# A decoder block on one core: two of three normalisations move to ScalarE, the split of the cross queries to GpSimd, the row of maxima to the head of VectorE's step, and a stack's transfers to other places in SyncE's list

## The reference

```
x = x + attn(layernorm(x))            # 16 heads of 8 channels, rotary positions, causal
x = x + xattn(layernorm(x), context)  # 16 heads over 256 context tokens, then W_proj and bias
x = x + ffn(layernorm(x))             # 8 experts, 2 chosen per batch from the mean over tokens
layernorm(x) = (x - mean) / sqrt(var + 1e-5)
ffn: hmid = gelu(h @ w1[e] + b1[e]); y = hmid @ w2[e] + b2[e]; out += weight[b, e] * y
```

## Time and profile before

| | |
|---|---|
| median of 3 runs | 202.76 us |
| profiled execution | 200.95 us, span 199.2 us |
| mean granted clock of TensorE | 0.947 of full speed |
| busy: PE / PEld / DVE / ACT / POOL | 84% / 58% / 71% / 53% / 26% |
| chain that ended last | PE 50%, DVE 19%, DMA 15%, SPq 5% |

### The profile page before, as it was taken

The page is one execution under the profiler, slowest core; times in us unless marked ns, Lnnn a source line. Parts: engine busy times, 40 slices in busy tenths (PEclk is TensorE's granted clock), DMA queues, the critical chain, the costliest instruction groups (busy, mean ns, idle before and its releaser), DMA issues.

```text
span 199.2 us, 4411 instructions
## 1 busy us (share of the span) xinstructions
PE 166.8 (84%) x1500; PEld 116.1 (58%) x1508; DVE 140.7 (71%) x545; ACT 104.8 (53%) x222; POOL 52.3 (26%) x103
## 2 busy tenths in 40 slices
PE   0686195699599979989998998998998899799994
PEld 0343184485466755755764655654665556598984
DVE  2789299897347899799799889888968346525020
ACT  2132021257147656566566666766676657793451
POOL 7810005668800070030030030010115107126050
PEclk9999669589769999999999999999999999999999
DMA  5817660058227503322321321300340350170720
GB/s 150 238 35 175 164 173 18 3 148 184 70 82 196 184 25 104 110 69 58 109 82 49 98 95 35 90 0 3 113 130 3 100 143 0 17 224 26 229 66 26
DMA packets 23842, 19.05 MB, mean 96 GB/s; under 512 B 2364, under 2 KB 21820, under 8 KB 23100
## 3 DMA queue, kind: packets, MB, share of 16 engines
q1 hardware_dynamic: 22908, 17.79, 31.9%
q10 hardware_dynamic: 912, 0.98, 2.0%
HBM read 12.54 MB, written 2.49 MB: 75 GB/s over the span
## 4 chain that ended last, share of the span: by engine, by line
PE 50%; DVE 19%; DMA 15%; SPq 5%; issue 4%; POOL 3%; ACT 2%; POOLq 0%; DVEq 0%; ACTq 0%
PE psV L914 11%; PE psB L893 9%; PE psA L868 8%; DMA stackQ<-maxT 6%; DMA stackQ<-scratch 4%; DVE masked L623 4%; PE psA L958 4%; PE psM L923 3%; PE psA L975 3%; DMA stackK<-hid 3%; PE psV L975 3%; PE psM L933 3%; DVE stats L554 2%; DVE negmax L629 2%; SPq L402 2%
## 5 line engine op out<-in xcount | busy, mean ns | idle before, releaser
L753 ACT ACTIVATE E<-psB 128x512 f32<-128x512 f32 x112 | 62.3, 595 | 37.3 <-PE psB L893 15.7
L868 PE MATMUL psA<-stackK,stackQ 72*128 72x256 bf16 (+1 forms) x256 | 44.4, 277 | 11.8 <-DMA stackK<-hid 5.5
L893 PE MATMUL psB<-stackQ,stackK 74*128 74x256 bf16 (+1 forms) x256 | 42.2, 264 | 4.6 <-DMA stackQ<-maxT 3.8
L623 DVE CUSTOM_DVE_ANT_0 masked<-psA,row_mask 128x128 bf16<-128x128 f32 (+1 forms) x128 | 36.8, 352 | 11.8 <-PE psA L868 11.7
L629 DVE TENSOR_REDUCE negmax<-psA 128x2 f32<-128x512 f32 x64 | 39.7, 677 | 0.0
L868 PEld LDWEIGHTS psA<-stackK,stackQ 72*128 72x128 bf16 x256 | 23.0, 105 | 21.5 <-DMA stackQ<-scratch 8.6
L914 PE MATMUL psV<-E,V 128*9 128x256 f32 (+1 forms) x512 | 30.9, 359 | 0.2 <-ACT E L753 0.2
L893 PEld LDWEIGHTS psB<-stackQ,stackK 74*128 74x128 bf16 x256 | 22.0, 100 | 12.5 <-DMA stackQ<-maxT 5.6
L468 POOL TENSOR_SCALAR rstd<-mv 128x2 f32<-128x2 f32 x12 | 2.8, 236 | 89.1 <-DVE mv L558 88.9
L914 PEld LDWEIGHTS psV<-E,V 128*9 128x9 f32 x512 | 11.0, 90 | 14.4 <-issue 7.9
L761 ACT ACTIVATE oT<-psV 128x256 f32<-128x256 f32 x32 | 12.3, 384 | 7.9 <-PE psV L914 7.2
(11 more groups left out here) (111 smaller groups left out, 247.0 us busy)
## 6 DMA issues: line engine op xcount, KB each, us to landing
stackK<-scratch SPq DMA_DIRECT2D x18, 192.0 KB
stackQ<-hid SPq DMA_DIRECT2D x36, 64.0 KB
w1s<-w_dram SPq DMA_DIRECT2D x8, 258.0 KB, 2.8
w2s<-w_dram SPq DMA_DIRECT2D x8, 256.0 KB, 3.7
stackQ<-scratch SPq DMA_DIRECT2D x3, 576.0 KB
stackK<-hid SPq DMA_DIRECT2D x18, 64.0 KB
scratch<-hid SPq DMA_DIRECT2D x4, 192.0 KB, 3.7
scratch<-parts_ctx SPq DMA_DIRECT2D x4, 192.0 KB, 4.7
```

The costliest lines, as they stand in the source:

```text
L623: last = dve.tensor_tensor_reduce(out=masked[:, bank, i * keys:(i + 1) * keys], in0=scores[:, i, 0:keys], in1=row_mask[:, S - keys:S], sca ...
L753: act.activation(dst, psB[:, bank].rearrange("p (h q) -> p h q", h=dst.shape[1]), ACT.Exp, scale=SCALE).then_inc(b_taken, 1)
L868: last = pe.matmul(psA[:, bank, i * keys:(i + 1) * keys], stackQ[0:ROWS, b, h, t * P:(t + 1) * P], stackK[0:ROWS, b, h, 0:keys], start=Tru ...
L893: last = pe.matmul(psB[:, bank, i * n:(i + 1) * n], stackK[:, b, h, t * P:(t + 1) * P], stackQ[:, b, h, q0:S], start=(s == 1 or i == 0), s ...
```

## The change

1. `ln_apply` of the second and third normalisation (s > 0) moves from VectorE to ScalarE, as Identity(res * rstd + shift). GpSimd makes shift = -mean * rstd in two more operations on two columns, one ahead of rstd and one behind it. The first normalisation stays.
2. The cross queries are copied out of psM by ScalarE (new buffer qc) and split by GpSimd, four operations; VectorE's four go.
3. `max_rows` is cut in two. TensorE's turn (`max_turn`) stays behind the half's units. VectorE's split and SyncE's transfer (`max_rows`) come ahead of them.
4. `o_turn`, `o_back`, `o_proj`, `ln_stats` and `ln_apply` come one half earlier; `ln_turn`, `q_cross`, `stack_read_k` and the routing keep their half.
5. Writes and reads of the stacks of batches 2 and 3 are steps of their own for keys and queries. The third batch's keys are written ahead of the first row of maxima, and both stacks are read ahead of the second batch's row of maxima.
6. The masked scores have two buffers instead of three.

```diff
--- before.py
+++ after.py
...
@@ -95,6 +95,7 @@
     put(5, "qk_self", 0, 3)
     put(6, "v_cross", 1, 1)
     put(7, "ctx_turn", 1, 2)
+    put(7, "max_turn", 0, 0)
     put(7, "max_rows", 0, 0)
...
@@ -102,9 +103,14 @@
...
-    put(9, "stack_write", 0, 2)
-    put(10, "stack_read", 0, 2)
-    put(14, "stack_write", 0, 3)
+    put(6, "stack_write", 0, 2, 1)
+    put(9, "stack_write", 0, 2, 0)
+    put(9, "stack_read", 0, 2, 1)
+    put(10, "stack_read", 0, 2, 0)
+    put(13, "stack_write", 0, 3, 1)
+    put(14, "stack_write", 0, 3, 0)
+    put(14, "stack_read", 0, 3, 1)
+    put(15, "stack_read", 0, 3, 0)
...
@@ -114,24 +120,22 @@
         s, b = divmod(j, NB)
         n = 2 * NG * j
         if j > 0:
-            put(n + 2 * NG, "max_rows", s, b)
-        if j == 1:
-            put(n + 2 * NG + 1, "stack_read", 0, 3)
-        m = n + LAG + 10
+            row_of[n + 2 * NG] = (s, b)
+        m = n + LAG + 9
         put(m, "o_turn", s, b)
         put(m + 1, "o_back", s, b)
         put(m + 2, "o_proj", s, b)
         put(m + 2, "ln_stats", s + 1, b)
         put(m + 3, "ln_apply", s + 1, b)
-        put(m + 4, "ln_turn", s + 1, b)
+        put(m + 5, "ln_turn", s + 1, b)
         if s == 0:
-            put(m, "stack_read_k", 1, b)
-            put(m + 5, "q_cross", 1, b)
-            put(m + 5, "stack_fill", 1, b)
+            put(m + 1, "stack_read_k", 1, b)
+            put(m + 6, "q_cross", 1, b)
+            put(m + 6, "stack_fill", 1, b)
...
@@ -153,13 +157,17 @@
...
+        if half in row_of:
+            order.append(("max_rows", *row_of[half]))
         order += [step for _, step in sorted(units, key=lambda unit: unit[0])]
+        if half in row_of:
+            order.append(("max_turn", *row_of[half]))
...
@@ -224,7 +232,7 @@
-        masked = sb("masked", [P, NA, 2 * S], BF16)
+        masked = sb("masked", [P, 2, 2 * S], BF16)
...
@@ -237,6 +245,8 @@
+        qc = sb("qc", [P, 2, S])
+        shift = sb("shift", [P, NB, NT])
...
@@ -379,16 +390,17 @@
...
-                if kind == "stack_write" and s == 0:
-                    sp.wait_ge(parts_k_self[b], NPART)
-                    write_parts(0, b, 1, parts[:, b, 1], scr_k_self[b])
-                    sp.wait_ge(parts_q_self[b], NPART)
-                    write_parts(0, b, 0, parts[:, b, 0], scr_q_self[b])
-                if kind == "stack_read" and s == 0:
-                    sp.wait_ge(scr_k_self[b], 16)
-                    read_k(s, b)
-                    sp.wait_ge(scr_q_self[b], 16)
-                    read_q(s, b)
+                if kind == "stack_write":
+                    which = st["g"]
+                    sp.wait_ge((parts_q_self[b], parts_k_self[b])[which], NPART)
+                    write_parts(s, b, which, parts[:, b, which], (scr_q_self[b], scr_k_self[b])[which])
+                if kind == "stack_read":
+                    which = st["g"]
+                    sp.wait_ge((scr_q_self[b], scr_k_self[b])[which], 16)
+                    if which == 1:
+                        read_k(s, b)
+                    else:
+                        read_q(s, b)
...
@@ -465,9 +478,14 @@
             def rsqrt_var(n, b):
 
                 pool.wait_ge(var_ready, n + 1)
+                if n >= NB:
+                    pool.tensor_scalar(shift[:, b, :], mv[:, b, :, 0], -1.0, None, ALU.mult)
                 then(pool.tensor_scalar(rstd[:, b, :], mv[:, b, :, 1], EPS, None, ALU.add))
                 pool.tensor_tensor(rstd[:, b, :], rstd[:, b, :], neg_half[:, :], ALU.pow).then_inc(rstd_ready, 1)
                 pool.wait_ge(rstd_ready, n + 1)
+                if n >= NB:
+                    pool.tensor_tensor(shift[:, b, :], shift[:, b, :], rstd[:, b, :],
+                                       ALU.mult).then_inc(shift_ready, 1)
...
@@ -489,9 +507,12 @@
                 if kind == "q_cross":
+                    bank, k = misc[0]
+                    pool.wait_ge(misc_taken[bank], k)
+                    split(qc[:, b % 2], parts[:, b, 0], parts_q[b])
                     if b == 0:
                         pool.wait_ge(bproj_in, 16)
-                    pool.wait_ge(xn_ready, NB + b + 1)
+                    pool.wait_ge(xn_later, b + 1)
...
@@ -557,7 +578,7 @@
-                if kind == "ln_apply":
+                if kind == "ln_apply" and s == 0:
...
@@ -592,17 +613,6 @@
-                if kind == "q_cross":
-                    bank, k = misc[0]
-                    dve.wait_ge(misc_full[bank], k)
-                    qq, dst = rot[:, b % 2, 0, 0], parts[:, b, 0]
-                    dve.tensor_copy(dst[:, 0], psM[:, bank, 0:S]).then_inc(parts_q[b], 1)
...
@@ -738,6 +748,19 @@
+                if kind == "q_cross":
+                    bank, k = misc[0]
+                    act.wait_ge(misc_full[bank], k)
+                    if b >= 2:
+                        act.wait_ge(parts_q[b - 2], NPART)
+                    act.activation(qc[:, b % 2], psM[:, bank, 0:S], ACT.Copy).then_inc(misc_taken[bank], 1)
+                if kind == "ln_apply" and s > 0:
+                    n = st["norm"] - NB
+                    act.wait_ge(shift_ready, n + 1)
+                    for t in range(NT):
+                        last = act.activation(xn[:, b, t, :], res[:, b, t, :], ACT.Identity, bias=shift[:, b, t:t + 1],
+                                              scale=rstd[:, b, t:t + 1])
+                    last.then_inc(xn_later, 1)
...
```

More of the change, by code:

```diff
@@ L72, in plan @@
 def plan():
-    extra = {}
+    extra, row_of = {}, {}
     def put(half, *step):
@@ L399, in _ @@
                 if kind == "max_rows":
-                    sp.wait_ge(misc_taken[st["misc"][0][0]], st["misc"][0][1])
+                    bank, k = use[("max_turn", s, b)][0]
+                    sp.wait_ge(misc_taken[bank], k)
                     for i in range(2):
@@ L619, in _ @@
                             dve.wait_ge(row_mask_set, 1)
-                        if unit >= NA:
-                            dve.wait_ge(a_taken, unit - NA + 1)
+                        if unit >= 2:
+                            dve.wait_ge(a_taken, unit - 1)
                         for i in range(nh):
-                            last = dve.tensor_tensor_reduce(out=masked[:, bank, i * keys:(i + 1) * keys], in0=scores[:, i, 0:keys],
+                            last = dve.tensor_tensor_reduce(out=masked[:, unit % 2, i * keys:(i + 1) * keys], in0=scores[:, i, 0:keys],
                                                             in1=row_mask[:, S - keys:S], scale=-1.0, scalar=LARGEST,
@@ L810, in _ @@
                         pe.wait_ge(ident_set, 1)
-                    pe.wait_ge(xn_ready, st["norm"] + 1)
+                    if s == 0:
+                        pe.wait_ge(xn_ready, b + 1)
+                    else:
+                        pe.wait_ge(xn_later, st["norm"] - NB + 1)
                     turn(xn[:, b], bank).then_inc(misc_full[bank], 1)
```

17 lines of the change are left out of this document (6 added, 11 removed).

## The result

The changed kernel takes 210.95 us (median of 4 runs), the kernel before 203.08 us in the same comparison: ratio 1.0496, 95% interval 1.0431 to 1.0562. It is 5% slower; the ratio compares only the fast executions of each kernel and so isn't the ratio of the two medians. The forecast of 201.8 us and its range of 196 to 206 us both miss it. The profiled execution took 209.5 us, its span is 207.7 us. Times of one kernel scatter by 3 to 4%, with the clock (an execution of before with a mean granted clock of 0.974 took 197.91 us, one with 0.941 took 205.05), which is low in other stretches from one execution to the next; so what follows goes by stretches and by the clock in them, mostly from one profiled execution of each kernel.

What follows compares the result with a forecast made beforehand. TensorE and VectorE, both nearly full, were taken to make each other wait. Terms -6.7, +3.85 and +1.9 sum to -0.95 us on the profiled 200.95, giving a median of 201.8 us, range 196.0 to 206.0.

Steps and rivals of the forecast that it cites:

- Part 1: Steady periods: taking up the row of maxima first and moving work off VectorE gives -6.7 us.
- ScalarE's term: Steady periods: ScalarE's added work ahead of exponentials costs 0.3 us a period, six times, +1.8 us; bounds 0 and 7.
- a ScalarE that waits for GpSimd in every period: Steady periods: a sign named in advance that would show the forecast wrong; no size given.
- ScalarE as the new wait: Steady periods: ScalarE stands for the shift every period, halving the 6.7 us gain; 205.2 us, chance 0.11.
- the rows first: Steady periods: VectorE takes up turned rows 1.9 us sooner, so all six waits for rows go, -5.6 us.
- the bank: Steady periods: a transpose's wait for VectorE to free a psM bank goes, -0.9 us.
- half of the maxima's waits: Steady periods: half of 4.1 us of waits for VectorE's reductions goes, -2.0 us; bounds 0 and 4.1.
- the smallest rival: Whole kernel: TensorE's own work is the period, waits are only redistributed; within 1 us of before, 202.8, chance 0.05.
- Part 2: Early stacks: the second batch's row lands behind the fourth's reads, at 60.6 us, then lower clock; +3.85 us.
- the first rival: Early stacks: the row of maxima isn't held up, making part 2 -4.35; 193.6 us, chance 0.20.
- Part 3: Tail: ScalarE's last normalisation waits for its shift and delays Gelus, +2.35 us, less one 0.46 us wait: +1.9 us.
- the rival with 0.22: Tail: the clock falls after TensorE's pauses, costing 3.2 us; 205.0 us, chance 0.22.

Runs made afterwards that it cites:

- e5: The changed kernel with the two later normalisations still on ScalarE, but half a group later in its list: 201.37 us, ratio 1.0033.
- e2: The changed kernel with both later normalisations back on VectorE: 201.74 us, ratio 1.0102.
- e7: The kernel before with only the rows of maxima put first on VectorE: 198.42 us, ratio 0.9885.
- e13: The kernel before with the rows of maxima first and the output chain half a group sooner: 195.5 us, ratio 0.9761.
- e12: The changed kernel with the second batch's row ahead of the fourth's reads, later normalisations on VectorE, output chain timed as before: 198.53 us, ratio 0.9897.
- e1: The changed kernel with the fourth batch's key and query reads back behind the second batch's row of maxima: 204.54 us, ratio 1.0144.
- e11: The kernel before with only the change's writes and reads of the third and fourth batch's stacks: 204.86 us, ratio 1.0240.
- e6: The changed kernel with the second batch's row of maxima issued from ScalarE's queue instead of SyncE's: 208.66 us, ratio 1.0385.
- e3: The changed kernel with only the very last normalisation back on VectorE: 206.5 us, ratio 1.0275.
- e8: The changed kernel, second row ahead of the fourth batch's reads, normalisations on VectorE, first cross keys read behind the third row: 195.72 us, ratio 0.9615.

## Why the prediction was wrong

The sum failed in three terms. The place is right in all; parts 2 and 3 have the right mechanism and the wrong size, and part 1 has the wrong mechanism.

- **Part 1, ScalarE's term (+1.8): the step that failed most.** "I charge 0.3 us a period", for 0.88 us of work ahead of the exponentials. The work cost nothing (e5); the wait in front of it did, 4.7 us over the periods by e5 (95.42 against 100.16) and 3.8 by e2. The prediction named this as a sign of being wrong, "a ScalarE that waits for GpSimd in every period", and it came: eight times of eight. The rival "ScalarE as the new wait" had a chance of 0.11, on the argument that VectorE stood idle before its sum and so didn't lag. That looks at the wrong chain. From the projection to the shift there are VectorE's sum and statistics and four dependent GpSimd operations, 1.6 us in the tail's rows (183.48 to 185.07). ScalarE had nothing but one copy and an exponential or two in its list for that time. The point I had named ("over 1 us after ScalarE's copy") is nearly met: the copy ends at 119.76, the shift comes at 120.50, 0.74 us later, and that was enough.
- **Part 1, the rows first (-5.6), the bank (-0.9) and half of the maxima's waits (-2.0).** Together -8.5, and -9.0 with the 0.46 us; e2 and e5, without ScalarE's waits, measure -6.2 and -7.2 against before's 102.59, so the sum was too large by 2 to 3 us, and came that near by luck, since the attribution was wrong. The 5.6 us are waits of weight loads; the products stood for 3.8 (e7). The rows first alone give 1.25 us (e7): the waits move to the maxima, as the smallest rival said. The half group's shift of the output chain gives 2.6 us (e13) to 2.9 us (e12) in four periods, shown from both sides, and the prediction costed it at 0.46 us, in one place. Why it gives that much stays open: the trace names a wait for only part of it. It is a change of two numbers in the table, and I treated it as bookkeeping.
- **Part 2 (+3.85, measured +5.20, alone +4.9).** The mechanism is shown: e1 undoes it and wins 10 us, e11 does it alone. The step that fell short is the landing, and less so the clock. Counted from the second group, TensorE started the product 12.75 us after it instead of 10.75: +2.00 where I had +1.15 (the row landed at 62.54, or 61.4 with the start's 1.14 us taken off, inside my bounds of 59.5 to 61.8 but 0.8 behind the 60.6). From there to the sixth group it is +3.20, about the half of the 6.29 us of work at the lower clock, where I had 2.7. "The queue is worked off in order" was half of it: on another queue 3.6 us of the delay stay (e6). What the early stack is worth with the row put ahead is shown by one execution each: e1 takes 4.8 us less than before in this stretch, near the first rival's -4.35, and 2.7 less than e7, which keeps the old stacks, waits 1.73 us for the third and then has 3.5 us at the low clock. e13 keeps them too and takes 12.90 us without that wait, but it came to the stretch 2.2 us later than e7, so it shows no more than that a late start hides the wait.
- **Part 3 (+1.9, of it +2.35 behind the 32nd group, measured +4.65).** The mechanism is right: ScalarE's last normalisation costs 2.8 us (e3) where I had 2.35; without the low clock ScalarE waits 3.21 us for it (e1), where I had 3.3. That the projection is not sooner was right (6.44 us after the mark in e1, 6.49 before); here it came 7.83 us after it, behind sixteen sums at the low clock. Most of the rest is that clock, 1.6 us, the rival with 0.22, at half its price of 3.2: the stretch was 3.4 us long, not 6.4.
- **The cases weren't exclusive.** I gave the two slower rivals 0.33 together, as alternatives. Both happened, on top of the forecast's own sum: 201.8 + 3.35 + 3.2 = 208.4 us by my own prices, against the median of 210.95. The range ended at 206 since no case had both.
- **Not varied by itself:** the masked scores' two buffers, which the prediction put at nothing.

## What to carry to other kernels

When a step moves to an engine with an in-order list, first lay its input's arrival beside its place in that list; the engine's idle share says nothing, and one place later in the list was worth 4.7 us in the periods and 3.5 in the tail here, 1.6 of these the clock's. When a large transfer is issued sooner, list every small one that it passes: a row of two times 8 KB behind 1.1 MB of reads cost 10 us in its stretch (e1), another queue took off 4 us and left 3.6, and writing the data of the next large read first cost nothing. If a scheduler's numbers shift by one, cost that shift as an edit of its own, and let independent losses add in the range.

## What the runs showed of the hardware

- A transfer of 8 KB lands in 1.8 to 1.9 us with nothing ahead. Of a pair behind three key reads of 192 KB and a query read of 576 KB on its own queue the first lands after 6.3 us and the second after 7.2; of a pair issued from the other queue beside those reads, the first after 2.5 and the second after 5.5 (e6).
- In two waits of 6.6 to 6.9 us the granted clock fell to 0.50 before the wait was over and stayed there for 10.2 and 13.7 us, 6.5 and 8.6 of them with work (after, e11). After shorter waits it was low for 3.4 to 13.7 us; the same work took 1.6 us more with 3.4 us of it in the tail. In e8 the low stretch of 13.7 us had TensorE busy for 13.57.
- GpSimd's shift, from four operations on 128x2 elements, takes 1.6 us, of which the power is 0.73.
